# Lightning attention block in split fp32: one level of Strassen's algorithm for queries, keys and gates, and two batches per pass over the heads

## What is computed

```python
xn  = layernorm(x)                                    # x: (4, 512, 512)
q, k, v = split(silu(xn @ w_qkv.T))                   # 16 heads x 128 each
# per head, blocks of tokens: decayed causal scores and a running state
o   = (q * q_decay) @ kv + ((q @ k.T) * diag_decay) @ v
kv  = block_decay * kv + (k * k_decay).T @ v
out = norm_w * o * rsqrt(mean(o * o) + eps)           # over all 2048 head features
s   = (sigmoid(xn @ w_gate.T) * out) @ w_out.T
p   = softmax(xn @ router_w.T + router_b);  top 8 of 64
ffn = xn * sum(top) + top @ expert_bias
x   = x + s * silu(ffn)
```

## Time and profile before

| | |
|---|---|
| runs | 1160.07, 1159.57, 1159.91 us; median 1159.91 us |
| span of the profiled execution | 1158.1 us; its own time is not listed apart from the three runs |
| instructions | 17412 |
| PE busy | 1136.1 us, 98% |
| DVE, ACT, POOL busy | 493.9, 384.8, 100.6 us |
| HBM read, written | 34.26 MB, 4.19 MB |

### The profile page before, as it was taken

One profiled execution on the slowest core, in us unless ns is written; L12 is line 12 of the kernel. 1 busy time (PEld: TensorE's weight loads), 2 busy tenths in 40 slices (PEclk: granted clock), 3 DMA queues, 4 the chain that ended last, 5 costly groups with the idle time before them and its releaser, 6 DMA issues.

```text
span 1158.1 us, 17412 instructions
## 1 busy us (share of the span) xinstructions
PE 1136.1 (98%) x6736; PEld 1004.8 (87%) x6736; DVE 493.9 (43%) x900; ACT 384.8 (33%) x627; POOL 100.6 (9%) x90
## 2 busy tenths in 40 slices
PE   5999999999999999999999999999999999999996
PEld 5898888888888888888888888888888888888885
DVE  5554453233433243333342335333253233467758
ACT  5433252223422242222522224221342223443443
POOL 1000010000100000000100001000010000100002
PEclk9999999999999999999999999999999999999998
DMA  8100011000200010000100001100010000103322
GB/s 279 37 1 1 1 55 37 1 1 1 91 0 0 0 54 36 0 0 0 54 36 0 0 0 54 36 0 0 0 61 29 0 0 24 68 3 108 110 73 92
DMA packets 14737, 38.90 MB, mean 34 GB/s; under 512 B 2032, under 2 KB 2160, under 8 KB 13680
## 3 DMA queue, kind: packets, MB, share of 16 engines
q1 hardware_dynamic: 14704, 38.46, 9.7%
HBM read 34.26 MB, written 4.19 MB: 33 GB/s over the span
## 4 chain that ended last, share of the span: by engine, by line
PE 92%; DVE 4%; DMA 2%; issue 1%; SPq 0%; ACT 0%; DVEq 0%
PE proj_ps L287 19%; PE proj_ps L289 19%; PE proj_ps L288 19%; PE out_ps L287 5%; PE out_ps L289 5%; PE out_ps L288 5%; PE head_ps L376 5%; PE score_ps L354 4%; PE head_ps L379 4%; PE kv_ps L363 4%; PE turn_ps L348 2%; DMA land_v<-x_dram 1%; PE out_ps L302 1%; DMA norms<-norm_w_dram 1%; DVE acc L970 1%
## 5 line engine op out<-in xcount | busy, mean ns | idle before, releaser
L287 PE MATMUL proj_ps<-xt_hi,wqk_hi 128*128 128x512 f32 x512 | 208.4, 407 | 0.3 <-DVE wqk_lo L776 0.3
L289 PE MATMUL proj_ps<-xt_hi,wqk_lo 128*128 128x512 f32 x512 | 200.5, 392 | 0.0
L288 PE MATMUL proj_ps<-xt_lo,wqk_hi 128*128 128x512 f32 x512 | 200.0, 391 | 0.0
L752 POOL TENSOR_TENSOR acc_sq<-acc_sq,square 128x512 f32<-128x512 f32 x64 | 83.6, 1306 | 1032.3 <-ACT square L602 1032.3
L287 PE MATMUL proj_ps<-wv_hi,xt_hi 128*128 128x256 f32 (+1 forms) x512 | 148.9, 291 | 0.0
L289 PE MATMUL proj_ps<-wv_hi,xt_lo 128*128 128x256 f32 (+1 forms) x512 | 146.5, 286 | 0.0
L288 PE MATMUL proj_ps<-wv_lo,xt_hi 128*128 128x256 f32 (+1 forms) x512 | 146.4, 286 | 0.0
L852 DVE TENSOR_TENSOR acc<-acc,out_ps 128x512 f32<-128x512 f32 x112 | 77.0, 688 | 153.8 <-PE out_ps L289 153.8
L289 PEld LDWEIGHTS proj_ps<-xt_hi,wqk_lo 128*128 128x128 f32 x512 | 96.1, 188 | 21.0
L890 DVE SCALAR_TENSOR_TENSOR gate_lo<-gated,pair_small,gate_hi 128x512 fp32r<-128x512 f32 x64 | 79.6, 1243 | 79.4 <-ACT gate_hi L606 79.4
L287 PEld LDWEIGHTS proj_ps<-xt_hi,wqk_hi 128*128 128x128 f32 x512 | 96.7, 189 | 17.9 <-DVE wqk_lo L776 0.7
(11 more groups left out here) (183 smaller groups left out, 1669.9 us busy)
## 6 DMA issues: line engine op xcount, KB each, us to landing
land_a<-wqk_dram SPq DMA_DIRECT2D x8, 1024.0 KB, 4.8
land_v<-wv_dram SPq DMA_DIRECT2D x8, 512.0 KB, 5.0
land_a<-wg_dram SPq DMA_DIRECT2D x8, 512.0 KB, 3.3
land_a<-wo_dram SPq DMA_DIRECT2D x8, 512.0 KB, 4.4
land_a<-x_dram SPq DMA_DIRECT2D x16, 256.0 KB, 4.5
out_dram<-acc SPq DMA_DIRECT2D x16, 256.0 KB, 2.7
land_v<-x_dram SPq DMA_DIRECT2D x14, 256.0 KB, 4.6
acc<-x_dram SPq DMA_DIRECT2D x3, 1024.0 KB, 10.8
```

What stands on the lines that cost most here:

```text
L287: pe.matmul(dst, w_hi, m_hi, start=first, stop=False)
L288: pe.matmul(dst, w_hi, m_lo, start=False, stop=False)
L289: return pe.matmul(dst, w_lo, m_hi, start=False, stop=last)
L752: pool.tensor_tensor(cols_b, cols_b, square[:, :], ALU.add).then_inc(square_used, 1)
```

## The change

Batches are taken two at a time. A step now covers one head pair and two batches, so there are 16 steps: pairs 0 to 7 for batches 0 and 1, then pairs 0 to 7 for batches 2 and 3. Every weight is loaded and split twice.

For each group (queries and keys of head 0, of head 1, gates of both heads) the weights form a 2x2 block matrix (two outputs by two halves of the features), and the tokens another (two halves of the features by two batches). The group's four 128x512 results come from seven block products instead of eight, each 2 slices by 3 fp32r products: 42 where `project` had 48. The operands are the blocks themselves and four sums on either side. The sums are made on POOL, whose queue now also does every lo part of a weight. Partial results stay in three PSUM banks; DVE moves them to SBUF between products (`e1` to `e7`), and ACT's function follows in place. One bank each is left for values (`v_ps`), output tiles (`out_ps`), transposed keys and key-value products (`tk_ps`), scores and head output.

Other parts that change: the token blocks of batches 2 and 3 are made during step 0 through `gate_hi` and `gate_lo` and sent to DRAM (`spill`), and loaded back at the end of step 7 (`load_block`). Batches 0 and 1 are finished within step 8 (`close=True`), 2 and 3 behind step 15. Router logits are products of their own (64 columns) beside the values (256 columns). The two residual rows are a ring of two that both the feed-forward row and the residual add read.

```diff
-LAST = PAIRS - 1
+TILES = 2 * NCH
+LAST = 2 * PAIRS - 1
@@ PE
+            def block_product(ps, buf, wblk, xblk, first, last):
+                for k in range(2):
+                    w_h2, w_l2 = w_hi[:, buf, wblk, k, :], w_lo[:, buf, wblk, k, :]
+                    x_h2, x_l2 = xt_hi[:, xblk, k, :], xt_lo[:, xblk, k, :]
+                    pe.matmul(ps[:, :], w_h2, x_h2, start=first and k == 0, stop=False, skip_group_check=True)
+                    pe.matmul(ps[:, :], w_h2, x_l2, start=False, stop=False, skip_group_check=True)
+                    end = pe.matmul(ps[:, :], w_l2, x_h2, start=False, stop=last and k == 1, skip_group_check=True)
+                end.then_inc(prod, 1)
...
+                        for w_h2, w_l2, lo, hi in ((wv_hi, wv_lo, at, at + 256),) + (
+                                ((rw_hi, rw_lo, 256, 256 + NEXP),) if last else ()):
...
+            def step(bp, ss, odd, last=False, close=False):
+                p1(ss, QK0, g[0])
+                p2(ss, QK0, g[0])
+                kv_products(bp0, before, 1, 1, last=close)
+                p6(ss, QK0, g[0])
+                head_output(before, 1, 0)
+                p5(ss, QK0, g[0])
+                p7(ss, QK0, g[0])
+                head_output(before, 1, 1)
+                p4(ss, QK0, g[0])
+                p3(ss, QK0, g[0])
+                turn_and_score(ss, 0, 0)
+                v_fill(bp, ss, 0, last)
+                if last:
+                    v_fill(bp, ss, 1, last)
+                turn_and_score(ss, 0, 1)
+                output_tile(before, 0)
...
@@ ACT, step
+                take_square(before, 0, 1)
+                raw_hi(group(ss, QK1), buf[1])
+                decays(ss, odd)
+                if close:
+                    exp_scores(0)
+                act.preload_act_table(ACT.Silu)
+                act_c11(ss, QK0)
+                take_square(before, 1, 0)
...
@@ DVE, step, close
+                if close:
+                    sum0(1)
+                    scale0(0)
+                    row0(2)
+                add_output(bp0, before, 6)
+                e7(ss, QK1)
+                if close:
+                    sum0(2)
+                    scale0(1)
+                add_output(bp0, before, 7)
...
@@ DVE, step 0
+            e7(0, QK0)
+            row_stats(2)
+            row_stats(3)
+            decay_scores(0, 0, 0)
@@ ACT, step 0
+            values_hi(1)
+            raw_hi(3, 1)
+            take_fill(1, 8)
@@ SP
+            load_group(0, group(0, GATE), GATE)
+            for f in range(8):
+                spill(f)
+            load_group(1, group(1, QK0), QK0)
+            for f in range(8, 16):
+                spill(f)
...
+            def load_res(t):
+                if t >= 2:
+                    sp.wait_ge(summed, t - 1)
+                sp.dma_start(res_row[:, t % 2, :], x_t[t // NCH][:, t % NCH, :]).then_inc(res_in[t % 2], 16)
@@ POOL
+            def weight_sums(n):
+                a11, a12, a22, a21 = (land_a[:, i, :, :] for i in range(4))
+                done = 4 * n
+                pool.wait_ge(w_l, 2 * n + 1)
+                pool.tensor_tensor(a22, a21, a22, ALU.add).then_inc(w_sum, 1)
...
+            def finish0(t):
+                pool.wait_ge(scaled, t + 1)
+                dst = acc[:, t // NCH, t % NCH, :]
+                pool.tensor_tensor(dst, dst, res_row[:, t % 2, :], ALU.add).then_inc(summed, 1)
```

More of the change, by code:

```diff
@@ L530, in _ @@
+            for i in range(4, 8):
+                pe.wait_ge(acc_set, TILES * LAST + i - 3)
+                output_tile(LAST, i, tail_out[i])
         @block.scalar
         def _(act):
[L532 to L539 removed]
@@ new lines, in decays @@
+            def decays(ss, odd):
+                act.wait_ge(cols_set, ss + 1)
+                if not (isinstance(ss, int) and ss == 0):
+                    act.wait_ge(probs_set, 4 * ss)
+                    act.wait_ge(q_decayed, 4 * ss)
+                for h in range(2):
+                    head = pair_cols[:, odd, NEG + h:NEG + h + 1]
+                    act.activation(decay[:, h, 0, :], lag, ACT.Exp, scale=head)
+                    last = act.activation(decay[:, h, 1, :], query_pos, ACT.Exp, scale=head)
+                last.then_inc(decay_exp, 1)
@@ L720, in _ @@
[L720 to L727 removed]
+            raw_hi(0, 0)
+            for f in range(4):
+                take_fill(0, f)
+            values_hi(0)
+            root_std(1)
@@ new lines, in _ @@
+            act_c22(0, QK0)
+            act_c21(0, QK0)
+            act_c12(0, QK0)
+            take_k_rows(0, 0, 0, 0)
+            take_k_rows(0, 0, 0, 1)
+            raw_hi(2, 0)
+            act.preload_act_table(ACT.Sqrt)
+            root_std(2)
+            root_std(3)
+            act.preload_act_table(ACT.Silu)
+            act_c11(0, QK1)
+            for f in range(4):
+                take_fill(1, f)
+            sums_hi(2, 0)
+            act_c22(0, QK1)
+            take_fill(1, 4)
@@ new lines, in _ @@
+            sums_hi(3, 1)
+            take_fill(1, 13)
+            act_c21(0, GATE)
+            take_fill(1, 14)
+            act_c12(0, GATE)
+            take_fill(1, 15)
+            act.wait_ge(spilled[0], 32 * 8)
+            act.wait_ge(spilled[1], 32 * 8)
+            gate_high(0, 0, 0)
+            out_hi(0, 0)
+            with act.Fori(0, 3) as it:
+                for j in range(2):
+                    step(0, 2 * it + 1 + j, (1 + j) % 2)
+            step(0, PAIRS - 1, 1, last=True)
@@ L730, in _ @@
+            root_rms(1, tail_bias[3])
+            act.preload_act_table(ACT.Silu)
+            for t in range(4, 8):
+                silu_row(TILES + t, tail_row(t))
         @block.gpsimd
@@ new lines, in _ @@
+            e4(0, GATE)
+            e5(0, GATE)
+            take_fill(1, 12)
+            take_fill(1, 13)
+            take_fill(1, 14)
+            decay_scores(0, 1, 1)
+            states(0, 0, 1, 0)
+            e7(0, GATE)
+            take_fill(1, 15)
+            gate_low(0, 0, 0)
+            gate_head(0, 0, 1)
+            with dve.Fori(0, 3) as it:
+                for j in range(2):
+                    step(0, 2 * it + 1 + j, (1 + j) % 2, 2 * it + 2 + j)
+            step(0, PAIRS - 1, 1, 0, last=True)
```

2000 lines of the change are left out of this document (1200 added, 800 removed).

## The result

The changed kernel takes 1267.01 us in the median (1265.86 to 1268.52), 1.0921 times the kernel before (95% interval 1.0906 to 1.0937). The forecast was 1236 us. The profiled execution has a span of 1266.7 us, against 1234 in the forecast's sum.

A forecast was written before the change was run, and what follows sets the result against it. PE was taken to bound the kernel. Its work of 1092.4 us plus waits of 10, 51, 44, 7, 5 and 24.5 gave a span of 1234, so 1236 us median, 6.5% slower; range 1168 to 1275.

The forecast's parts named there:

- Products: PE's work: 2016 products of 512 columns instead of 2304, -66.1 us; logits split into 256 and 64 columns, +14 us.
- PE busy 1092: PE's busy time over the whole span: 1136.1 less saved products, plus transposes, logits and switches, giving 1092.4 us.
- the clock falls in the waits: Rival: each of some 8 waits over 5 us lowers PE's clock, up to 1.7 us each, +14, 1250 us; chance 0.12.
- Waits of the start, 51 us plus the first 10: Step 0: first transposes at 10 us, then 51 us of PE waits beside 64.4 of work; step 1 counts from 125.4.
- the first row of the table: Stretch from the start to step 1's first key transposes: forecast 125.4 + 13.4 = 138.8 us, measured 149.9.
- A plain step, "I book 0": The twelve plain steps: slack 0.3 to 1 us everywhere, so no PE waits booked and 65.2 us per step.
- POOL blocks DVE: Rival: meetings with POOL stop DVE, perhaps 1.5 us a step reaching PE, 15 x 1.5 = +22, 1258 us; chance 0.15.
- Step 8, 44 us: PE waits at the change of halves: late weights, router work on DVE, residual rows, and clearing before step 9; 44 us.
- the ring: Step 8: DVE waits for reloaded residual rows, ready 6.4 us after scaling; PE loses 6, 3, 7, 5, 3 us for rows 2 to 6.
- Tail, 45.5 us: From the last gate product to the end: 45.5 us, about 34 of DVE's own work; PE works 21, idles 24.5.
- Start and step 8 hide most waits: Rival, faster: queues run further ahead, waits in steps 0 and 8 under 15 us instead of 95; about 1138; chance 0.10.
- about half of these waits: Rival: only about half of the forecast PE waits occur, giving 1185 us; chance 0.15.

The follow-up runs named there:

- the kernel with busy waits: Changed kernel plus 153 extra 512-column products, results unread, filling seven of PE's waits in steps 0 and 8; ratio 1.0823 to the kernel before.

## Why the prediction was right, and where not

- **The side, and the mechanism.** Slower, because the products saved in plain steps are less than the waits added at the ends of the halves. That is right: most of the large stops stood where they were put, released by what was named. The size was short by 31 of 107 us, and it was not worse because waits 13 us too long stood against work on PE 46 us too short.
- **The signs named in advance.** Come true: plain steps of 65.2 to 66 us in eight of twelve, 2016 products, 9.68 us before scores (0,1) released by DVE, step 8 not under 85 us (102.75). Not come true: PE busy near 1092 (1138.2); step 1 counted from 120 to 130 us (149.9 less 13.4 is 136.5); four to six waits of 4 to 6 us for `res_row` (six, but only two over 4); 20 us or more on DVE after PE's last product, which ends at 1254.4 where DVE ends at 1264.2. Plain steps over 67 us, the sign for contention, came four times, and from the loops.
- **Products.** 3 groups of lines with 672 each, 2016 as forecast; three products of 256 and three of 64 columns take 0.69 us together (553.48 to 554.17) where three of 320 took 0.44, so 64 x 0.25 = 16 in place of 14. Most starts of 64-column products lie 0.11 us apart (553.75 to 553.86 in the timeline), as the one-column row had it; the second of each three starts only 0.03 after the first, but the 256-column product behind them then takes 0.20 us to the next start (553.97 to 554.17) and not 0.12. The trace has a weight load for each product, and these start every 0.11 to 0.12 us throughout. By the floor of near 25 ns that the Trainium skill gives ("TensorE: Matmul & The Clock Gate", Back-to-back issue gap) the logits would have cost nothing; the trace disagrees where each small product loads its own weights.

```profile
553.72 0.19 PE L432 MATMUL v_ps<-rw_hi,xt_hi 128*128 128x64 f32 x1
553.75 0.27 PE L433 MATMUL v_ps<-rw_lo,xt_hi 128*128 128x64 f32 x1
553.86 0.28 PE L434 MATMUL v_ps<-rw_hi,xt_lo 128*128 128x64 f32 x1
```

- **PE busy 1092.** Measured 1138.2. The 12 plain steps hold 791 of it, 9 more than 12 x 65.2; the other 37 are in the start, steps 7 and 8, and the end. The mean granted clock of the execution is 0.965, so it spent 2 x 0.035 x 1266.7 = 89 us at the lower level. PE was busy for 56 of them (its busy time in the windows whose granted clock is 0.50), and work in that time takes double: 28 of the 46 us are the clock's. 2 more are the logits; the rest I cannot split. The rival "the clock falls in the waits" came true as a mechanism. Its price, 14, was asked of the wrong rows (1.97 us for eight transposes say nothing of the work after them), and what the clock costs in time is another question again: filling seven of the waits took away a third of the 89 us and won 6.5.
- **Waits of the start, 51 us plus the first 10.** Measured idle time of PE to 149.9: 55.7 us, against 61; its busy time 94.2, against 64.4 + 13.4. So the waits were 5 too long and the work 16 too short. Half of these 16 are the clock: PE was busy for 17 us in this stretch's windows at 0.50. This failed step (work at full clock plus waits) is the 11 us of the first row of the table, and in steps 7 and 8 it hid behind waits that were too long.
- **A plain step, "I book 0".** The term that failed most, 22 of the 33 us by which the span exceeds the sum: "slack 0.3 to 1 everywhere", and "contention: I book nothing, since they stand where there is slack". A clean step is 65.95 where 65.2 was forecast, and the 0.75 is explained: 0.52 is the query decay behind POOL, 0.23 goes with the loops written out. Without both it is 65.20. The rival "POOL blocks DVE" was the right mechanism at a third of its price (0.52 us a step for 1.5). The reading that spoke against it, a lo part "hardly touched", was wrong: it had been held until POOL was done. In the changed kernel 26 of the 64 lo parts are held likewise (1.4 us for 0.69), and yet PE does not wait in a plain step once the query decay is moved (in that kernel it is busy for 65.18 of 65.18 us).
- **Loop edges, not in the forecast.** 12 plain steps take 804.3 us for 782.4. 6 of these 22 are the query decay, 15 to 16 the loops (13 by the ratio). The trace of before had no row that shows them, and they should have been bounded all the same: the change writes new loops.
- **Step 8, 44 us.** With 3.5 us for step 7's values these are the 47.5 against 32.0 of idle time. The parts: the ring costs 12 to 14 and not 24; the add of tile 0 costs nothing and not 3; the change to step 9 stops PE for 5.35 and 5.53 us where 12 was forecast, the second for another reason than forecast: the weights queued behind eight stores on SyncE (7 us), not POOL's clearing. I had walked SyncE's queue for step 8's weights, and not for step 9's.
- **Tail, 45.5 us.** From the last gate product it is 51 us; step 15 before it was shorter by about as much, which is luck again. DVE works through the end without a gap, as forecast.
- **"Start and step 8 hide most waits" and "about half of these waits"** fall: PE is idle 128.5 us.

## What to carry to other kernels

An algorithm with fewer products pays only where PE is full, and here it is in 12 of 16 steps; this kernel, full from end to end before, lost more at its new start, middle and end together than one product in eight gave back. Price a seam by walking every queue across it, SyncE's loads for the step after the seam included, and expect that taking away one wait shows the next. When an experiment comes out at the number that was expected, look where in the span the time went before you believe the cause.

## What the runs showed of the hardware that I had not expected

- Behind a stop of 4 us or more PE works at the lower clock for some us, and at one loop edge behind two stops of 1.21 and 1.96 us with four products between them: 0.43 us from start to start for 512 columns, 0.23 otherwise.
- At the edges of PE's loops a step is 1.5 to 6.2 us longer, the clock's fall among it. In the kernel with busy waits three of four edges were gone, though its loops were the same; in the one with the eighth product the edges of the first half cost 6.4 and 6.7 us (76.38 and 76.67 against 70.02).
- A DVE operation with two SBUF operands of 512 columns that starts during one of POOL ends 0.55 us after POOL's end, whatever its own start (64 lo parts in the kernel before), one of 384 columns 0.42 us after, where POOL's operation has two tensor operands; the additions and evacuations that read PSUM beside POOL keep their 0.69 us. Where every instance of an operation is held, its mean looks like its own length.
